# A row shift moved from VectorE to ScalarE, and shorter inverse roots, in a transformer block of delta-rule attention and routed experts

## The reference

```python
mod = silu(c) @ wmod                           # sa, ca, ga, sb, cb, gb for each batch
h = layernorm(x) * (1 + ca) + sa
x = x + ga * attn(h)                           # delta rule: recurrence over 256 rows, k normed by rsqrt,
                                               # output normed by rsqrt(mean(o*o) + eps), then Wo
h = layernorm(x) * (1 + cb) + sb               # layernorm: (x - mean) / sqrt(var + eps)
x = x + gb * moe(h)                            # top 1 of 8 experts, silu(a) * g, times the top probability
```

## Time and profile before

| what | value |
|---|---|
| device time, median of 3 runs | 593.61 us (592.37 to 595.03) |
| the profiled execution | 596.38 us |
| its span | 594.6 us |
| VectorE (DVE) busy | 465.2 us, 78% |
| TensorE (PE) busy | 392.0 us, 66% |
| GpSimd (POOL) busy | 307.3 us, 52% |
| ScalarE (ACT) busy | 262.1 us, 44% |
| granted TensorE clock, mean | 0.829 |

### The profile page before, as it was taken

One profiled execution on the slowest core, in us unless ns is written; L12 is line 12 of the kernel. 1 busy time (PEld: TensorE's weight loads), 2 busy tenths in 40 slices (PEclk: granted clock), 3 DMA queues, 4 the chain that ended last, 5 costly groups with the idle time before them and its releaser, 6 DMA issues.

```text
span 594.6 us, 9205 instructions
## 1 busy us (share of the span) xinstructions
PE 392.0 (66%) x2675; PEld 356.0 (60%) x2675; DVE 465.2 (78%) x1240; ACT 262.1 (44%) x549; POOL 307.3 (52%) x399
## 2 busy tenths in 40 slices
PE   3837534459913997645095865669867789997790
PEld 2312104459913996644094855559857788997780
DVE  5959899999999966999999999975565623547643
ACT  2885956322402312435355625263443354564440
POOL 1134135669999729854755838812152375332231
PEclk9978965678775897977587977698989987999995
DMA  7338889700000000920210001115100012133105
GB/s 188 66 66 102 110 112 145 65 2 2 0 0 2 0 2 1 356 69 0 42 30 2 1 2 36 33 36 107 42 24 23 23 51 73 54 113 86 49 24 150
DMA packets 50033, 34.00 MB, mean 57 GB/s; under 512 B 10960, under 2 KB 46560, under 8 KB 49984
## 3 DMA queue, kind: packets, MB, share of 16 engines
q1 hardware_dynamic: 46976, 28.01, 24.7%
q0 software_dynamic: 3008, 5.40, 2.9%
HBM read 14.21 MB, written 10.26 MB: 41 GB/s over the span
## 4 chain that ended last, share of the span: by engine, by line
DVE 38%; issue 21%; PE 18%; POOL 13%; DMA 5%; ACT 4%; SPq 1%; POOLq 0%; DVEq 0%; ACTq 0%
DVE U L1330 6%; DVE S L1344 6%; POOL placed_y L858 5%; POOL sorted_h L816 5%; PE bank L665 4%; PE bank L514 3%; PE bank L481 2%; DVE p L1325 2%; PE bank L681 2%; POOL prod_o L257 2%; DVE p L1337 2%; PE bank L530 2%; DVE K L1437 1%; DVE X L1288 1%; DVE big L1286 1%
## 5 line engine op out<-in xcount | busy, mean ns | idle before, releaser
L514 PE MATMUL bank<-prod_o,ID 128*128 128x128 f32 x512 | 80.6, 323 | 65.0 <-ACT K L1006 27.4
L514 PEld LDWEIGHTS bank<-prod_o,ID 128*128 128x128 f32 x512 | 74.9, 232 | 66.7 <-POOL prod_o L262 28.5
L257 POOL TENSOR_TENSOR prod_o<-Q,S 128x256 f32<-128x256 f32 x112 | 92.6, 856 | 33.0 <-PE bank L518 25.9
L858 POOL DMA_INDIRECT placed_y<-Q,place x46 | 44.7, 971 | 118.9 <-DVE Q L1518 115.2
L665 PE MATMUL bank<-Q,p 128*128 128x128 f32 x736 | 100.5, 284 | 0.5 <-DVE Q L1504 0.5
L665 PEld LDWEIGHTS bank<-Q,p 128*128 128x128 f32 x736 | 94.2, 200 | 1.4 <-issue 1.1
L999 ACT ACTIVATE p<-S,GAM 128x64 f32<-128x64 f32 x126 | 49.5, 411 | 77.4 <-DVE S L1344 77.4
L1119 ACT ACTIVATE p<-big 128x1024 f32 x46 | 48.5, 1056 | 70.1 <-PE bank L665 69.7
L1344 DVE TENSOR_REDUCE S<-p 128x64 f32<-128x320 f32 x126 | 54.6, 472 | 10.0 <-issue 10.0
L530 PE MATMUL bank<-big,ID 128*128 128x128 f32 (+3 forms) x256 | 42.7, 343 | 28.0 <-POOL big L775 28.0
L530 PEld LDWEIGHTS bank<-big,ID 128*128 128x128 f32 x256 | 42.1, 238 | 29.3 <-POOL big L775 29.1
(11 more groups left out here) (216 smaller groups left out, 753.6 us busy)
## 6 DMA issues: line engine op xcount, KB each, us to landing
big<-in_L_ffn_w_dram SPq DMA_DIRECT2D x1, 4096.0 KB, 13.1
big<-big SPq DMA_DIRECT2D x16, 192.0 KB, 4.9
Q<-sorted_h SPq DMA_DIRECT2D x46, 64.5 KB, 1.9
sorted_h<-ZERO SPq DMA_DIRECT2D x2, 1472.0 KB, 16.9
X<-in_L_attn_x_dram SPq DMA_DIRECT2D x8, 256.0 KB, 4.3
big<-big SPq DMA_DIRECT2D x16, 128.0 KB, 4.7
X<-Q SPq DMA_DIRECT2D x32, 64.0 KB, 2.5
K<-placed_y SPq DMA_DIRECT2D x8, 256.0 KB, 3.2
```

Source lines behind the costliest of these rows:

```text
L257: engine.tensor_tensor(slot[:, 0:HD, m, :, :], q, s_, ALU.mult)
L514: pe.matmul(ps, ID[:, :], prod_o[:, k % 2, i, :], start=(i == 0), stop=False, skip_group_check=True)
L858: pool.indirect_dma_start(placed_y[g // NF], bass.IndirectOffsetOnAxis(ap=place[:, g:g + 1], axis=0), YS[:, g % YR, :], None).then_inc(sem ...
```

## The change

The four shift groups of slice 0 go from VectorE's order to ScalarE's, at the same `n` and behind the same waits. Those of slice 1 stay on VectorE. In the roots, the copy that only carried a signal goes; the instruction ahead of it signals. The Newton step y(1.5 - 0.5 y^2 v) takes two fused instructions in place of three.

```diff
+            def shift_rows(k):
+                act.wait_ge(sem("xn2t_ps"), k + 1)
+                if k >= 2:
+                    act.wait_ge(sem("h2_ps"), k - 1)
+                for i in range(4):
+                    b = 4 * k + i
+                    act.activation(H2T[:, k % 2, i * P:(i + 1) * P], TURN_BANKS[0][k][:, i * P:(i + 1) * P], ACT.Identity,
+                                   scale=MOD[:, 3, b:b + 1], bias=MOD[:, 2, b:b + 1]).then_inc(sem("shifted"), 1)
...
                 if AT_ROWS < n <= AT_ROWS + 4:
                     scale_rows(n - AT_ROWS - 1)
+                if AT_SHIFT <= n < AT_SHIFT + 4:
+                    shift_rows(n - AT_SHIFT)
                 if AT_SHIFT + 2 <= n < AT_SHIFT + 6:
                     rows(n - AT_SHIFT - 2)
...
-            def ask_root(var, t):
+            def ask_root(ins):
                 roots[0] += 1
-                dve.tensor_copy(t, var).then_inc(sem("root_in"), 1)
+                ins.then_inc(sem("root_in"), 1)
                 dve.wait_ge(sem("root_in"), roots[0])
...
                 link(dve.reciprocal(y, sroot))
                 link(dve.tensor_tensor(t, y, y, ALU.mult))
-                link(dve.tensor_tensor(t, t, var, ALU.mult))
-                link(dve.tensor_scalar(t, t, -0.5, 1.5, ALU.mult, ALU.add))
-                dve.tensor_tensor(y, y, t, ALU.mult).then_inc(sem("roots_ready"), 1)
+                link(dve.scalar_tensor_tensor(out=t, in0=t, scalar=-0.5, in1=var, op0=ALU.mult, op1=ALU.mult))
+                dve.scalar_tensor_tensor(out=y, in0=t, scalar=1.5, in1=y, op0=ALU.add, op1=ALU.mult).then_inc(sem("roots_ready"), 1)
...
-                link(dve.tensor_scalar(ve[:, :], mv[:, :, 1], LN_EPS, None, ALU.add))
-                ask_root(ve[:, :], y2[:, :])
+                ask_root(dve.tensor_scalar(ve[:, :], mv[:, :, 1], LN_EPS, None, ALU.add))
...
-                if AT_SHIFT <= n < AT_SHIFT + 4:
-                    shift2(n - AT_SHIFT)
```

More of the change, by code:

```diff
@@ L1228, in key_norms @@
                 link(dve.tensor_reduce(n2, slice_rows(K_[h], s), AX_X, ALU.add))
-                link(dve.tensor_scalar(n2, n2, K_EPS, None, ALU.add))
-                ask_root(n2, t_)
+                ask_root(dve.tensor_scalar(n2, n2, K_EPS, None, ALU.add))
             def unit_keys(h, s):
@@ L1352, in sums_of_squares @@
                     dve.wait_ge(sem("sqo_used"), s + 1)
-                    link(dve.tensor_scalar(ms, ms, 1.0 / HD, O_EPS, ALU.mult, ALU.add))
-                    ask_root(ms, sm[:, 5, :])
+                    ask_root(dve.tensor_scalar(ms, ms, 1.0 / HD, O_EPS, ALU.mult, ALU.add))
             def stats2(q):
```

## The result

The changed kernel takes 597.24 us (median of 20 runs, 595.14 to 599.37), the kernel before 594.01 beside it (20 runs, 591.15 to 597.74). The ratio is 1.0046, 95% interval 1.0028 to 1.0064: half a per cent slower. Forecast were 587.7 us and 583.8 to 592.5, so both the sign and the range were wrong.

What follows compares the result with a forecast made beforehand. VectorE, busiest of the engines, was taken to bound the kernel. Roots 4.16 plus shift 1.75 gave 5.9 us off the profiled 596.38, so 590.5; with the median 0.5% below that execution, 587.7 us, range 583.8 to 592.5.

Steps and rivals of the forecast that it cites:

- Does TensorE allow this?: Shift steps n = 49 to 52: the last transpose is ready before ScalarE asks at 337.7, with 0.8 us to spare.
- the 1.75: Shift steps n = 49 to 52: ScalarE becomes the bound and the last state starts 1.75 us earlier, not 5.0.
- The root's 1.11: Rows' root of slice 0, ahead of the recurrence: dropping the copy and shortening the Newton step saves 1.11 us.
- The shift's price on ScalarE: Moved shift groups: four shifts take 1.45 us on ScalarE, against 1.35 on VectorE.
- VectorE would no longer pace these steps: Steps n = 49 to 52: ScalarE paces them, VectorE idles some 3 us in sum ahead of the state's reduce.
- the scatter moves with VectorE: GpSimd's scatter ahead of the sorted tiles: it shifts with VectorE; route to first tile changes by 0.
- The sum was 4.16: All ten roots, over the whole kernel: the shorter forms together save 4.16 us.
- Memset to aggregate, 1.56 forecast: Roots of keys and of slice 0's outputs: savings of 0.39 + 0.52 + 0.65 us.
- The tile stage, 1.07 forecast: First tile to end, roots of slice 1's outputs and rows: savings of 0.65 + 0.42 us.
- The rule on fused operations: Fused root operations: the skill's half rate was set aside, pricing them like tensor_tensor; by it the sum is about 1.9 smaller.
- D: Rival, shift steps: waits keep TensorE at its lower clock, ScalarE blocks 8.6 us; 596.3 us, slower; chance 0.06.
- C: Rival: no change to speak of; the shift gains 0, a wait joins each group, 1.8 us remain; 591.8 us; chance 0.22.

Runs made afterwards that it cites:

- set 3: Runs of the changed kernel, roots alone, the two ScalarE blocks exchanged, and the changed kernel with a VectorE delay; the kernel before takes 594.19 us there.
- e2_shift: Only the shift moved to ScalarE, roots as before, against the kernel before: 592.81 us, ratio 0.9995.
- e5: The changed kernel again, nothing else altered, against the kernel before at 616.30 us: 612.79 us, ratio 0.9948.
- e9: The changed kernel a third time, against the kernel before at 594.19 us: 596.36 us, ratio 1.0042.
- e13: The changed kernel a fourth time, against the kernel before at 617.50 us: 611.78 us, ratio 0.9921.
- e17: The changed kernel with six linked memsets (some 2 us) on VectorE, against the kernel before at 616.89 us: 616.55 us, ratio 0.9989.
- e1_roots: Only the ten roots changed, shift left on VectorE, against the kernel before: 590.65 us, ratio 0.9962.
- e3_before_warm: The kernel before plus 30 idle TensorE matmuls in the tiles, against the kernel before: 591.89 us, ratio 0.9977.
- e4_full_warm: The changed kernel plus the same 30 idle TensorE matmuls in the tiles, against the kernel before: 589.47 us, ratio 0.9931.
- the delayed kernel: The changed kernel plus six memsets (some 2 us) on VectorE behind the first tile's copy: 593.37 us in its one run.
- sets 2 and 4: Repeats of the changed kernel, rows first (also with idle matmuls) and delayed versions; the kernel before takes 616.30 and 617.50 us, the changed one 612.79 and 611.78.
- set 1: Roots alone, shift alone, and the kernel before and the changed kernel each with idle matmuls; the kernel before takes 592.97 us.

## Why the prediction was wrong

**The failed step is "Does TensorE allow this?"** It took TensorE's timetable from the trace of before, where the last transpose stands at 336.28, and compared it with ScalarE's new one. That timetable hangs on ScalarE itself. The second half of each router but the first waits until `rows` of the group before has left the one bank that slice 0's back-transposes share, `pe.wait_ge(sem("h2_evac"), k)`. In ScalarE's new order `rows` of one group stands behind the shift of the next but one. So the shift that was moved there, 1.5 us, is itself what TensorE waits for: 1.56 and 1.29 us. The last transposes, in TensorE's queue behind the first wait, are late, and ScalarE waits 1.89 us for them with the decay behind it. The last logits stand behind the second wait, and the route waits 1.35 us for them; the prediction had them no later than the state. The four steps get 1.07 us longer instead of 1.75 shorter. The experiment that exchanges the two blocks shows the cause: 19.78 us instead of 23.12, both in set 3, and both waits all but gone. The text had named `rows` as dear to delay and still did not ask who waits for it.

**What the 3.4 us from aggregate to route are made of.** The waits alone, read from `e2_shift`, leave 0.55 of the 1.75: 1.2 us. The root's 1.11 did not reach the route in the changed kernel: TensorE's second transpose starts 14.42 us behind the aggregate as with the shift alone and its old roots, since the sums of outputs ahead of it ran longer at the lower clock (3.62 and 1.41 us against 3.50 and 0.98). And the lower clock at the last logits took 1.06. The first of the three is shown by the exchange. The other two are differences of single profiles; that of the logits has the same size (1.71 or 1.72 for L586) in four other profiles with TensorE's first wait at 1.55 us (`e5`, `e9`, `e13` and `e17`, whose delay comes later), and no run was made that holds the clock up in these steps.

**What held in this part.** The shift's price on ScalarE (1.45 forecast, 1.48 to 1.51 measured). The estimate of 1.55 by the Trainium skill, ScalarE: Activation LUTs, What ACT_TABLE_LOAD costs, lies about as close to this trace. That VectorE would no longer pace these steps: it waits ahead of the state's reduce, 4.5 us in sum and 2.6 with rows first. The size of the gain, 1.75 forecast, is 2.31 once the order is right. That the scatter moves with VectorE: route to first tile 50.27 and 50.28, with the last batch again long, 5.36.

**The roots: a term each, too large.** The sum was 4.16; roots alone give 2.3 (0.38% of 593). Memset to aggregate, 1.56 forecast: the three profiles of the table with the old roots have a mean of 220.96, the seven with the new ones 219.61, so 1.35 came, though the seven spread from 218.66 to 220.34. At the rows' root, 1.11 forecast: 1.18 and 1.30 came with roots alone (7.54 to 6.36 and 6.24), but 0.56 in the profile of the changed kernel, where all three fused operations take 0.71 (the last two take 0.33 and 0.28 in `e1_roots`). The same kernel shows both forms (6.98 and, delayed much later in the program, 6.28), so this is a matter of how VectorE's small operations fall against GpSimd's products in one execution. In the six timelines compared (before, roots alone twice, changed twice, delayed) the operations behind the root's third take 0.23 to 0.34 where GpSimd has just begun its 128x128 products (L262), and 0.71 where its 128x256 products (L257) still run. The tile stage, 1.07 forecast: at an equal clock 197.77 and 197.69, so 0.1 came. The error there is that of crediting in full a saving on VectorE in a stage where TensorE's products and their clock set the pace.

**The rule on fused operations.** The last two instructions of a root take 0.29 us each at 128 elements and 0.42 to 0.43 at 256, as the tensor_tensor did. By the Trainium skill, Vector Engine (DVE) Microarchitecture Reference, Points that are easy to get wrong, they would run at half rate; this trace does not agree.

**The tiles, a term that the sum did not have.** 1.84 us were lost from the first tile to the end, 2.59 of them (and more than all) in four tiles at a granted clock of 0.79. That the clock is what costs there is shown by `e3_before_warm` and `e4_full_warm`: matmuls that do nothing bring the clock to 1.00, the four tiles to 20.6 and 20.9 us, and put the changed kernel below the kernel before. That the edit lowers the clock there is not shown. Why the same gap of 2.86 us leaves TensorE at the upper level in one execution and at the lower in another stays open. The moment of the gap, counted from the start, does not decide: behind it the first matmul comes at 470.75 in the delayed kernel, with eight matmuls in 1.06 us, and at 470.78 in the changed one, with 1.92. Nor does the kernel: the two profiles of the roots alone have 1.06 and 1.92.

**The rivals.** D forecast 596.3 us, near the result of 597.24, and partly by luck. It had TensorE at the lower clock up to the last transpose, for 8.6 us of ScalarE's time. In the changed kernel the clock there is 1.00 as before, and the transpose was late because TensorE waited for ScalarE. But what D named did happen behind that: after a wait for ScalarE the clock fell, at the last logits for 1.06 us, and in `e4_full_warm` and the delayed kernel already ahead of the last transpose. Its other half, that ScalarE blocked at the transposes holds the decays, is what happened. C's "a wait joins each group" is near the mechanism too, and it was priced at a gain of 0 as its worst.

**The sign depends on the set.** In sets 2 and 4 the same change is 0.5 to 0.8% faster. What differs there is the stop of 17 to 18 us inside the four tiles, where the changed kernel lost its time at the low clock. That the stop hides this loss is only argued: no run takes the stop away, and there is no profile of the kernel before from these sets.

**The better version.** Rows ahead of the shift is faster than the change in each of three sets: 593.26 against 596.36, 608.96 against 612.79, 609.34 against 611.78. Against the kernel before it is 0.3% faster in set 3 (0.9940 to 0.9999), barely clear of no change and no better than the roots alone, and 1.2 and 1.3% in sets 2 and 4. Its first tile is 2.8 us ahead of that of the roots alone in set 3 (386.74 and 389.52), and the tiles give this back. The change with idle matmuls has 0.9931 in set 1. Both together were timed only where the kernel before takes 617 us, at 0.988 to 0.990.

## What to carry to other kernels

When work is put into an engine's queue, go through each thing that then stands behind it there and ask on the other engines who waits for that. Above all, look whether the timetable that the moved work itself needs (here TensorE's transposes) is among them; taking that timetable from the old trace assumes the answer. Where two small blocks can stand in either order, the one that another engine waits for goes first: here that alone turned a loss of 0.4% into a gain of 0.3%. Two parts timed alone need not add up either (0.9962 and 0.9995 against 1.0046 together). And a gain ahead of a stage whose clock rises and falls is not sure to arrive: compare that stage at an equal granted clock before crediting or blaming an edit.

## What the runs showed of the hardware

* Four tiles take 20.6 us at a granted TensorE clock of 1.00 and 25.5 at 0.77. Thirty idle matmuls kept it up in `e3_before_warm` and `e4_full_warm`. Two profiles of one kernel (roots alone) differ there by 2.1 us, at 0.94 and 0.83.
* Short waits of TensorE came ahead of falls of its clock in the shift's steps: eight matmuls of the router's logits took 0.96 us at 1.00 and 1.72 behind a wait of 1.29, sixteen of the sum of outputs 1.95 and 2.89 behind a wait of 1.90. The same wait of 1.29 left the clock at 1.00 in `e2_shift`.
* A VectorE operation on 16 elements takes 0.17 us undisturbed and up to 0.71 while GpSimd multiplies; a fused one can be stretched as far as a plain one (0.71 each in one execution, 0.33 and 0.28 in another), so fusing need not save anything there.
* The kernel before takes 593 to 594 us in some sets and 616 to 617 in others, whole sets at a time. In the latter three engines are nearly idle for 18 us in the tiles, with no releaser on the core. The ratio of the same two kernels was 1.004 in the former and 0.992 to 0.995 in the latter.
